# Row maxima over 512 and 234 columns instead of two halves of 373, the short parts of two query tiles in one bank and one instruction

## The reference

```python
h = _L0_tok_ref(x, ...)                                   # (16, 746, 128)
h = h + _L0_attn_ref(_layernorm(h, axis=-1), ...)         # 8 heads of 16
h = h + _L0_ffn_ref(_layernorm(h, axis=-1), ...)          # 8 experts, top 1, hidden 512

# in the attention
scores = jnp.einsum('bhqd,bhkd->bhqk', qp, kp) * scale
probs = jax.nn.softmax(scores, axis=-1)
attn = jnp.einsum('bhqk,bhkd->bhqd', probs, vp)
```

## Time and profile before

| | before |
|---|---|
| median of 3 runs | 1277.85 us (1277.65 to 1279.09) |
| span of the profiled execution | 1275.9 us (its own device time beside the span is not given) |
| PE busy | 1178.7 us, 92% |
| DVE busy | 1072.5 us, 84% |
| ACT busy | 950.6 us, 75% |
| POOL busy | 680.0 us, 53% |
| L1112, the reductions, 1536 | 760.8 us of DVE |
| L1247, maxima quads, 6144 matmuls | 519.1 us of PE |
| L1247, score quads of 32 weight columns, 6144 matmuls | 515.7 us of PE |
| mean granted TensorE clock | 0.965 of full speed |

### The profile page before, as it was taken

How to read it: one execution, slowest core, us unless ns; L and a number is a source line. 1 busy time by engine, 2 the same in 40 slices (tenths; PEclk the granted TensorE clock), 3 DMA queues, 4 the chain that set the end, 5 groups by cost and what they waited for, 6 DMA issues and landing times.

```text
span 1275.9 us, 53879 instructions
## 1 busy us (share of the span) xinstructions
PE 1178.7 (92%) x21379; PEld 745.5 (58%) x21379; DVE 1072.5 (84%) x2756; ACT 950.6 (75%) x2477; POOL 680.0 (53%) x894
## 2 busy tenths in 40 slices
PE   6479999999999999999999999999999846899996
PEld 3334656555555556555555556565644326899996
DVE  7469899999999999999999999999999544577774
ACT  4426988888887878788888878797877824567774
POOL 2062436566473837475665739374723334456664
PEclk9768999999999999999999999999999969899998
DMA  8152132222313131323223131313220513333331
GB/s 190 39 84 79 40 86 72 76 84 61 94 52 94 45 105 42 104 72 79 83 63 93 51 94 45 106 41 104 72 80 28 150 56 105 88 93 105 103 101 50
DMA packets 79409, 102.32 MB, mean 80 GB/s; under 512 B 15916, under 2 KB 72995, under 8 KB 78734
## 3 DMA queue, kind: packets, MB, share of 16 engines
q1 hardware_dynamic: 70624, 79.02, 23.4%
q0 software_dynamic: 8384, 20.22, 5.1%
q10 hardware_dynamic: 186, 0.02, 0.0%
HBM read 60.76 MB, written 38.93 MB: 78 GB/s over the span
## 4 chain that ended last, share of the span: by engine, by line
PE 63%; DVE 20%; issue 5%; POOL 3%; ACT 2%; DMA 1%; SPq 1%; another core or an unknown queue 1%; POOLq 0%; DVEq 0%; ACTq 0%
PE psum L1247 36%; DVE half_max L1112 14%; PE psum L1312 13%; PE psum L1391 6%; PE psum L1401 5%; PE psum L1252 2%; ACT arena L808 2%; DVE stats L916 1%; POOL out_dram L720 1%; DVE rows L990 1%; PE psum L1382 1%; POOL arena L405 1%; DMA arena<-max_rows 1%; PE psum L1267 1%; DVE arena L962 1%
## 5 line engine op out<-in xcount | busy, mean ns | idle before, releaser
L1112 DVE TENSOR_REDUCE half_max<-psum 128x1 f32<-128x373 f32 x1536 | 760.8, 534 | 62.8 <-PE psum L1247 55.0
L808 ACT ACTIVATE arena<-psum 128x373 f32<-128x373 f32 (+1 forms) x1536 | 655.0, 489 | 154.4 <-PE psum L1247 139.0
L1247 PE MATMUL psum<-k_rows,arena 96*32 96x373 bf16 x6144 | 519.1, 329 | 14.9 <-DVE half_max L1112 6.1
L1247 PE MATMUL psum<-arena,k_rows 98*32 98x373 bf16 x6144 | 515.7, 326 | 13.7 <-ACT arena L808 6.2
L1312 PE MATMUL psum<-arena,values 128*32 128x373 f32 (+1 forms) x3072 | 313.2, 478 | 0.2
L1247 PEld LDWEIGHTS psum<-k_rows,arena 96*32 96x32 bf16 x6144 | 173.8, 96 | 195.7 <-DVE half_max L1112 103.4
L1247 PEld LDWEIGHTS psum<-arena,k_rows 98*32 98x32 bf16 x6144 | 176.4, 95 | 178.2 <-ACT arena L808 74.8
L631 POOL DMA_INDIRECT routed_rows_dram<-rows,pos_i x96 | 96.6, 1007 | 170.7 <-PE psum L1247 106.2
L720 POOL DMA_INDIRECT out_dram<-arena,slot_id x101 | 119.2, 1180 | 90.0 <-issue 51.5
L1312 PEld LDWEIGHTS psum<-arena,values 128*32 128x32 f32 (+1 forms) x3072 | 98.4, 110 | 20.7 <-issue 2.8
L861 ACT COPY arena<-psum 128x128 f32<-128x128 f32 x101 | 26.9, 266 | 77.7 <-PE psum L1382 39.7
(11 more groups left out here) (218 smaller groups left out, 1447.5 us busy)
## 6 DMA issues: line engine op xcount, KB each, us to landing
arena<-q_parts_dram SPq DMA_DIRECT2D x192, 93.2 KB, 2.4
k_rows<-k_parts_dram SPq DMA_DIRECT2D x192, 93.2 KB, 2.4
arena<-routed_rows_dram SPq DMA_DIRECT2D x101, 130.0 KB
q_parts_dram<-q_part SPq DMA_DIRECT2D x48, 186.5 KB, 2.3
k_parts_dram<-k_part SPq DMA_DIRECT2D x48, 186.5 KB, 2.0
arena<-in_x_t_dram SPq DMA_DIRECT2D x3, 703.1 KB, 14.1
seq<-in_w_dram SPq DMA_DIRECT2D x1, 2048.0 KB
seq<-in_w_dram SPq DMA_DIRECT2D x8, 256.0 KB
```

The costliest lines, as they stand in the source:

```text
L808: nc.scalar.activation(probs[0:kn(kt), G % N_P, j, :], st_bank[s % N_ST][0:kn(kt), 0:HALF], ACT.Exp).then_inc(s_exp, 1)
L1112: nc.vector.tensor_reduce(half_max[:, m:m + 1], mx_bank[m % N_MX][:, 0:HALF], AX.X, ALU.max)\
L1247: last = nc.tensor.matmul(dst[n:n + m], weights[:, n:n + m], moving, start=start, stop=stop)
```

## The change

The 746 columns of a query tile are cut into 512 and 234 instead of 373 and 373. The work of four steps (two query tiles of one head) becomes three units: 512 columns of the first tile, 512 of the second, and the 234 columns of both side by side in one bank, reduced by one instruction into two columns of `half_max`. They run in steps 0, 1 and 2 of each four; the fourth has no maxima quad and no reduction. `half_max` keeps its layout, so what follows it is untouched. `s_mx` and `s_red` now count units, 72 to a sequence. A third unit is two quads with one signal behind the second.

```diff
+    WIDTH = 512
+    REST_W = L - WIDTH
+    GROUP_UNITS = 3
+    UNITS = GROUPS * GROUP_UNITS
...
-        def maximum_of(i, s):
+        def unit_of(i, s):
 
-            return (i, s + LEAD) if s + LEAD < STEPS else (i + 1, s + LEAD - STEPS)
+            b, m = (i, s + LEAD) if s + LEAD < STEPS else (i + 1, s + LEAD - STEPS)
+            return (b, m // GH * GROUP_UNITS + m % GH) if m % GH < GROUP_UNITS else (-1, 0)
...
                 if n == 0:
-                    dve.wait_ge(s_red, b * STEPS + STEPS // 2 * (g + 1))
+                    dve.wait_ge(s_red, b * UNITS + UNITS // 2 * (g + 1))
...
-                    b, m = maximum_of(i, s)
+                    b, u = unit_of(i, s)
                     if 0 <= b < B:
-                        dve.wait_ge(s_mx, b * STEPS + (m + 1))
-                        nc.vector.tensor_reduce(half_max[:, m:m + 1], mx_bank[m % N_MX][:, 0:HALF], AX.X, ALU.max)\
-                          .then_inc(s_red, 1)
+                        dve.wait_ge(s_mx, b * UNITS + (u + 1))
+                        first = u // GROUP_UNITS * GH
+                        if u % GROUP_UNITS < 2:
+                            m = first + 2 * (u % GROUP_UNITS)
+                            nc.vector.tensor_reduce(half_max[:, m:m + 1], mx_bank[u % N_MX][:, 0:WIDTH], AX.X, ALU.max)\
+                              .then_inc(s_red, 1)
+                        else:
+                            nc.vector.tensor_reduce(
+                                half_max[:, first:first + GH].rearrange("p (t a) -> p t a", a=2)[:, :, 1],
+                                mx_bank[u % N_MX][:, 0:2 * REST_W].rearrange("p (t n) -> p t n", t=2), AX.X, ALU.max)\
+                              .then_inc(s_red, 1)
...
+            def unit(dst, b, h, t, low, high):
+
+                return quad(dst, q_rows[b % 2][0:KR, h, D * t:D * (t + 1)], k_rows[b % 2][0:KR, h, low:high])
...
-                    pe.wait_ge(s_red, B * STEPS)
+                    pe.wait_ge(s_red, B * UNITS)
...
-                    b, m = maximum_of(i, s)
+                    b, u = unit_of(i, s)
                     if 0 <= b < B:
 
-                        h, t, half = m // 12, m % 12 // 2, m % 2
-                        if m % 48 == 0:
-                            pe.wait_ge(s_ld[m // 48], b * 192 + 192)
-                        wait(pe, s_red, b * STEPS + (m + 1 - N_MX))
-                        quad(mx_bank[m % N_MX][:, 0:HALF], q_rows[b % 2][0:KR, h, D * t:D * (t + 1)],
-                             k_rows[b % 2][0:KR, h, half * HALF:(half + 1) * HALF]).then_inc(s_mx, 1)
+                        h, pair, part = u // 9, u % 9 // GROUP_UNITS, u % GROUP_UNITS
+                        if u % 36 == 0:
+                            pe.wait_ge(s_ld[u // 36], b * 192 + 192)
+                        wait(pe, s_red, b * UNITS + (u + 1 - N_MX))
+                        if part < 2:
+                            last = unit(mx_bank[u % N_MX][:, 0:WIDTH], b, h, 2 * pair + part, 0, WIDTH)
+                        else:
+                            for t in range(2):
+                                last = unit(mx_bank[u % N_MX][:, REST_W * t:REST_W * (t + 1)], b, h, 2 * pair + t,
+                                            WIDTH, L)
+                        last.then_inc(s_mx, 1)
```

## The result

The changed kernel takes 1282.95 us (median of 20 runs, 1278.78 to 1285.29), the kernel before beside it 1277.66 us (20 runs). The ratio is 1.0042, 95% interval 1.0033 to 1.0051: slower by 5 us, where 27 us less were forecast. A repetition in a later series gave 1.0034 (1.0022 to 1.0046).

A forecast was written before the change was run, and what follows sets the result against it. PE was taken as nine tenths busy, with DVE's lateness costing it 37.0 us. Winning 26 us of that, plus half of 0.9 early on, gave a span of 1249.4, or 1251 us as median; range 1236 to 1273.

The forecast's parts named there:

- DVE's fixed part, banks, pitches: VectorE's maxima reductions: each group saves one fixed part, 0.063 us (1.748 instead of 1.812), 24 us of DVE's time in all.
- The spare of a bank: Time before PE wants a maxima bank again: from 0.28 to 0.66 us, 0.38 more for DVE's work between reductions.
- The sum: Late maxima quads, about five bursts a body: 1.7 of 2.4 us a body won, 26 us of DVE's 37.0.
- The residual come[s] no later than before: DVE's residual, small reduction and casts: no later than before, since their last unit is now a step earlier.
- I take nothing for PE: TensorE's maxima quads: same columns and weight loads, short quads 0.105 us, no change in PE's time; bounds 0 and 4 us.
- The rival of the short quads: Weight loads stop hiding behind PE's short quads: PE pays 45 us, wins 26, giving 1297 us; chance 0.06.
- Rival 1: PE sooner waits for ACT, DVE stays 94% busy; only DVE's stretches of the chain shrink, 6 us, 1272; chance 0.18.
- The sign named last in the prediction: A sign of being wrong: late score quads on PE take over what the maxima quads give back; no size given.

## Why the prediction was wrong

- **DVE's fixed part, banks, pitches: right in the main.** Reductions of 681 and 636 ns, long quads 0.22, pairs 0.20. In runs a reduction starts 0.61 us (long behind long), 0.60 (pair behind long) and 0.56 (long behind pair) after the one before, 1.77 a group against 1.748 forecast and 1.812 before: 0.04 us saved, not 0.063. The spare of a bank did what was worked out: late maxima quads fell from 29.8 to 6.2 us where about a third of 33 was expected to stay. The busy time of the reductions fell by 11 us, not 24.
- **The sum: this step failed.** "A burst is shortened by the new spare of 0.38 at most, the shorter ones vanish" took each late quad as time won once it is early. DVE's lag isn't gone, only unseen by the banks: PE may now run up to a whole group ahead, and it meets DVE at the next place that needs one of DVE's other results. The first such place is step 41, where 8 of the 24 us came back; moving the residual ahead of it won them (1.0034 to 0.9970). The term that was wrong is the 26 us of the sum.
- **"The residual come[s] no later than before": wrong.** The unit of step 38 is now the pair, whose signal comes behind two quads; and PE, no longer held by banks, is early. 0.3 us of waiting became 0.9 in each of 14 bodies. Moving the residual won 8 us in the changed kernel, nothing in the old one. The late transposes also start the DMA of the maxima rows late (13.3 to 20.6 us of waits), which fits part of the 3.9 us by which score quads grew.
- **"I take nothing for PE": right for a short quad, wrong for the stream.** The rival of the short quads named the sign but another mechanism, weight loads, at another price. What came were 12.4 us of stops inside the pair behind HTOK, and undoing that meeting alone won 4 to 5 us.
- **Rival 1, the stalls only move,** is the nearest to what happened, with the price wrong: it left 6 us of gain. With the gaps alone undone the kernel stands at 1.0003, so the join and the order took that gain as well. The sign named last in the prediction, late score quads that take over, shows in part: 19.4 to 23.3 us, and more with the pair first.
- The balance of PE's lateness: 23.6 us less at maxima quads; against them 12.7 more inside maxima quads and pairs, 8.2 at MAX, 3.9 at score quads, 3.7 at and inside the weighing and PROJ, and 3.3 in smaller places. In all 8.2 more (60.0 to 68.2); bodies grew by 0.3 us, some 5 us over 15.5 of them.

**What stays open:** what in PE's instruction path makes the gaps. They sit at the same place of the program, last some 0.7 us, often come twice some eight to ten records apart, and don't follow the loads' DMA traffic. A dense stretch of records (HTOK has 54, the pair 16) isn't enough: the second HTOK has the same and no stop. Where they were seen a scatter of POOL was just starting; that was not varied. That the instructions arrive late would fit; no row shows it. The remaining 0.4% of the pair's place are measured, not explained beyond 3 us at MAX. And of the 27 us forecast some 17 are missing even with both costs undone; that they went into waits for ACT and the maxima rows is read from the waits, not shown by an edit.

## What to carry to other kernels

A wait that disappears is won time only up to the next place where the same two engines meet. Before counting it, list these joins (shared banks, results that the faster engine needs) and ask by how much the slower engine is behind there; move its step ahead of the join together with the change. Where a dense stretch of small instructions runs through a queue, look how many more a reordering puts right behind it, and what the other engines start at that moment; compare with a place where the same instructions pass without a stop.

## What the runs showed of the hardware

- PE stops of about 0.7 us without any semaphore, in the midst of four matmuls, behind 66 records in 0.87 us (515.99 to 516.85) and within 0.15 us of the start of a scatter on POOL or some 0.8 us behind it; 27 idle times of PE without a releaser in the changed kernel from 110 to 990 us, 8 with the pair first, 2 with HTOK in fewer records, 2 in the kernel before. The same records without a scatter that starts at the pair pass without a stop.
- A reduction over two strips of 234 columns with a strided output takes 636 ns, one over 512 takes 681: 45 ns less for 44 columns less (468 against 512).
- 24 fp32 matmuls of 8 columns in four column groups start within 0.21 us, 9 ns each. The Trainium skill ("TensorEngine Tiling (Array Packing)", Instruction Overhead) gives each matmul some 60 cycles, 25 ns at 2.4 GHz; in this trace matmuls that go round four column groups start closer than that.
